# Cross-attention's product with the values in three fp32r passes, the scaling of the probabilities on GpSimd, ScalarE and VectorE reordered

## The reference

```python
q = jnp.einsum('bsd,hdk->bhsk', queries, Wq)      # queries = layernorm(x), 16 heads of 64
k = jnp.einsum('bsd,hdk->bhsk', keys, Wk)         # keys = values = ctx, (4, 77, 256)
v = jnp.einsum('bsd,hdv->bhsv', values, Wv)
scores = jnp.einsum('bhsk,bhtk->bhst', q, k) / jnp.sqrt(DK)
scores = jnp.where(mask[:, None, :, :] == 0, NEG, scores)
weights = jax.nn.softmax(scores, axis=-1)
out = jnp.einsum('bhst,bhtv->bhsv', weights, v)
x = x + out.transpose(0, 2, 1, 3).reshape(B, S, H * DV) @ Wo
```

## Time and profile before

| | us |
|---|---|
| median of 3 runs (lowest to highest) | 1695.28 (1693.06 to 1700.02) |
| the profiled execution, and its span | 1694.84, 1693.1 |
| TensorE, VectorE, ScalarE, GpSimd busy | 1646.5, 1379.5, 1089.0, 401.5 |
| self-attention | 70 to 750 |
| cross-attention, first scores to the last product's start | 846.3 to 1163.4 |
| experts, from the first matmul | 1176.0 to 1693.1 |

### The profile page before, as it was taken

One profiled execution on the slowest core, in us unless ns is written; L12 is line 12 of the kernel. 1 busy time (PEld: TensorE's weight loads), 2 busy tenths in 40 slices (PEclk: granted clock), 3 DMA queues, 4 the chain that ended last, 5 costly groups with the idle time before them and its releaser, 6 DMA issues. The chain is left out here.

```text
span 1693.1 us, 34421 instructions
## 1 busy us (share of the span) xinstructions
PE 1646.5 (97%) x11830; PEld 1086.5 (64%) x11830; DVE 1379.5 (81%) x2604; ACT 1089.0 (64%) x2271; POOL 401.5 (24%) x464
## 2 busy tenths in 40 slices
PE   7899999999999999999999999997999999999998
PEld 3443333333333333358689999996898888888887
DVE  6799999999999999925678899995797666666664
ACT  5348888888888888862577877774335444454442
POOL 2000000000000000023042222222562555555550
PEclk9869999999999999999999999998999999999999
DMA  6602111111111111021311322113725333333335
GB/s 208 211 16 37 34 33 33 31 31 32 31 31 31 31 31 31 3 63 56 122 49 39 109 77 69 52 47 129 236 75 172 57 54 54 56 52 57 51 57 172
DMA packets 85176, 116.80 MB, mean 69 GB/s; under 512 B 19051, under 2 KB 64415, under 8 KB 84415
## 3 DMA queue, kind: packets, MB, share of 16 engines
q1 hardware_dynamic: 67248, 90.95, 19.2%
q0 software_dynamic: 13728, 18.88, 6.8%
q10 hardware_dynamic: 4047, 4.91, 1.0%
HBM read 71.25 MB, written 46.60 MB: 70 GB/s over the span
## 5 line engine op out<-in xcount | busy, mean ns | idle before, releaser
L506 DVE TENSOR_REDUCE half_max<-psA 128x1 f32<-128x512 f32 x1024 | 630.3, 683 | 6.5 <-PE psA L559 4.4
L538 ACT ACTIVATE PT<-psB 128x1024 f32<-128x1024 f32 x512 | 520.4, 1026 | 140.4 <-PE psB L569 140.1
L559 PE MATMUL psA<-KS,QS 48*128 48x512 f32 x1024 | 397.6, 471 | 7.9 <-PEq L104 2.0
L569 PE MATMUL psB<-QS,KS 50*128 50x512 f32 x1024 | 377.8, 457 | 0.1
L588 PE MATMUL psO<-PT,VG 128*32 128x256 f32 x4096 | 321.0, 392 | 0.1
L559 PEld LDWEIGHTS psA<-KS,QS 48*128 48x128 f32 x1024 | 163.4, 191 | 232.5 <-DVE half_max L506 174.2
L588 PEld LDWEIGHTS psO<-PT,VG 128*32 128x32 f32 x4096 | 84.6, 108 | 176.4 <-issue 102.9
L1390 ACT ACTIVATE x_probs<-x_scores,x_neg_max 128x77 f32<-128x77 f32 x512 | 176.3, 357 | 6.7 <-DVE x_neg_max L1293 6.5
L2129 ACT ACTIVATE swd_high<-WD 128x1024 fp32r x71 | 75.3, 1061 | 149.9 <-PE m_psY L1872 149.9
L569 PEld LDWEIGHTS psB<-QS,KS 50*128 50x128 f32 x1024 | 150.9, 186 | 10.7 <-ACT PT L538 9.5
L1872 PE MATMUL m_psY<-swd_high,m_hT 128*128 128x256 f32 x760 | 155.6, 288 | 0.3 <-issue 0.2
(11 more groups left out here) (232 smaller groups left out, 2690.6 us busy)
## 6 DMA issues: line engine op xcount, KB each, us to landing
QS<-q_parts SPq DMA_DIRECT2D x96, 128.0 KB
q_parts<-part SPq DMA_DIRECT2D x16, 512.0 KB, 4.3
mx_kept<-cx_mx SPq DMA_DIRECT2D x8, 616.0 KB, 4.9
cx_mx<-mx_kept SPq DMA_DIRECT2D x4, 1232.0 KB, 7.4
KS<-k_parts SPq DMA_DIRECT2D x32, 128.0 KB
xf_rows<-XF SPq DMA_DIRECT2D x32, 128.0 KB, 1.7
acc<-X SPq DMA_DIRECT2D x32, 128.0 KB, 1.8
xf_turned<-n_xfT SPq DMA_DIRECT2D x32, 128.0 KB, 1.8
```

The costliest lines, as they stand in the source:

```text
L506: dve.tensor_reduce(half_max[:, h * (TB // 2) + t % (TB // 2), n:n + 1], psA[:, bank_of(slot, 2 * v + r), :], axis=AX.X, op=ALU.max).then_ ...
L538: act.activation(PT[:, k % 4, 2 * a:2 * a + 2, :].rearrange("p h n -> p (h n)"), psB[:, u % 2, :, :].rearrange("p a n -> p (a n)"), ACT.Ex ...
L559: pe.matmul(psA[:, bank_of(slot, m), :], QS[top:top + KQ, slot, h // 2, t * P:(t + 1) * P], KS[top:top + KQ, slot, n * HALF:(n + 1) * HALF ...
L569: mm = pe.matmul(psB[:, u % 2, r, :], KS[top:top + KM, slot, c * P:(c + 1) * P], QS[top:top + KM, slot, a, half * HALF:(half + 1) * HALF], ...
```

## The change

1. The product with the values takes high and low parts: `ET[0]`, `ET[1]` (ScalarE's copy, and VectorE's subtraction from PSUM) and `VO[..., part]`, both fp32r, in three passes: high x high, high x low, low x high. The third waits for the low parts (`e_low`).
2. `VO` holds two sequences at a time. In `phase_context` the values of sequences 2 and 3 are copied raw to `VR` (10 units, in turns), and those of 0 and 1 split, the high part by ScalarE, the low one by VectorE behind it (10 units). In `phase_cross` GpSimd splits `VR` into the slot that is free, one or two chunks a step in seven steps, from step 13 on and again from step 21 on.
3. GpSimd scales the probabilities (`scale_probs`): eight heads after VectorE's first reciprocal, eight after its second (`head_sums`), both calls in a row, behind the splitting and ahead of `n_rstd_all`. GpSimd's steps are all unrolled.
4. The softmax scale goes into the keys; the maximum is written negated and taken in the step of the scores, so the small negation goes.
5. VectorE's order in a step: `x_xnT` low ahead of the masked copies; then the low parts of `x_ET`, reciprocal, maximum, `XF`, its statistics, reciprocal. ScalarE: the first six exponentials ahead of the copies `n_xfT` and `x_xnT`, and `x_xnT` ahead of the copies to `x_ET`.
6. `XF` has two buffers in place of 32 and waits for its store and transposition of two tiles ago; the experts' high weights that lay in its place get one of their own.

The diff, cut to its core:

```diff
 phase_context
+        BACKS = [(b, pair) for b in (2, 3, 0, 1) for pair in range(NPK // 2)]
+        RAW = 2 * (NPK // 2)
@@ VectorE
-            for n in range(1, BACK, 2):
+            for n in range(1, RAW, 2):
                 dve.wait_ge(r_done, n + 1)
-                to, source = back(n)
-                dve.tensor_copy(to, source).then_inc(r_in[1], 1)
+                dve.tensor_copy(raw(n), back(n)).then_inc(r_in[1], 1)
+            for n in range(RAW, len(BACKS)):
+                dve.wait_ge(r_in[0], n - RAW // 2 + 1)
+                dve.tensor_tensor(part_of(n, 1), back(n), part_of(n, 0), ALU.subtract).then_inc(r_in[1], 1)
@@ ScalarE
+            for n in range(0, RAW, 2):
+                act.wait_ge(r_done, n + 1)
+                act.activation(raw(n), back(n), ACT.Copy).then_inc(r_in[0], 1)
             act.wait_ge(mx_in, MX_KEPT)
-            for n in range(0, BACK, 2):
+            for n in range(RAW, len(BACKS)):
                 act.wait_ge(r_done, n + 1)
-                act.activation(to, source, ACT.Copy).then_inc(r_in[0], 1)
+                act.activation(part_of(n, 0), back(n), ACT.Copy).then_inc(r_in[0], 1)
 phase_cross
@@ GpSimd
+            def scale_probs(t, half):
+                i, e = t
+                first, last = HEADS[half]
+                pool.wait_ge(recip_done, 2 * i + half + 1)
+                probs = by_head(PX, e)[:, first:last, :]
+                pool.tensor_tensor(probs, probs, over_keys(recip[:, e, first:last]), ALU.mult).then_inc(scaled, 1)
+            def split_values(slot, c):
+                n = slot * NPK + c
+                pool.tensor_copy(VO[:, slot, 0, c, :], VR[:, slot, c, :]).then_inc(vo_split, 1)
+                pool.wait_ge(vo_split, 2 * n + 1)
+                pool.tensor_tensor(VO[:, slot, 1, c, :], VR[:, slot, c, :], VO[:, slot, 0, c, :], ALU.subtract).then_inc(vo_split, 1)
...
+                own_rstd(0, L_Y)
+                if t := tile(L_Y):
+                    slot, j = t[0] // TB - 1, t[0] % TB
+                    if slot in (0, 1) and j < SPLIT_STEPS:
+                        if j == 0:
+                            pool.wait_ge(y_done, TB * (slot + 1))
+                        for c in range(j * NPK // SPLIT_STEPS, (j + 1) * NPK // SPLIT_STEPS):
+                            split_values(slot, c)
+                if t := tile(L_SM):
+                    scale_probs(t, 0)
+                    scale_probs(t, 1)
+                own_rstd(1, L_XF)
@@ TensorE
-                    pe.wait_ge(scaled, at(i, 1, 1))
+                    pe.wait_ge(scaled, at(i, 2, 2))
...
-                    for c in range(NPK):
-                        if c % 4 == 0:
-                            pe.wait_ge(e_in, at(i, 3, c // 4 + 1))
-                        mm = pe.matmul(psY[:, 0, 0:D], ET[:, c, :], VO[:, i // TB, c, :], start=(c == 0), stop=(c == NPK - 1))
+                    for a, b in PRODUCTS:
+                        for c in range(NPK):
+                            if c % 4 == 0 and (a, b) != PRODUCTS[1]:
+                                pe.wait_ge(e_low if a else e_in, at(i, 3, c // 4 + 1))
+                            mm = pe.matmul(psY[:, 0, 0:D], ET[a][:, c, :], VO[:, slot, b, c, :], ...)
@@ VectorE
+            def head_sums(t, half):
+                i, e = t
+                first, last = HEADS[half]
+                dve.wait_ge(exp_done, at(i, XH, last))
+                dve.reciprocal(recip[:, e, first:last], row_sum[:, e, first:last]).then_inc(recip_done, 1)
...
-                    dve.reciprocal(recip[:, :], row_sum[:, e, :]).then_inc(recip_done, 1)
-                    dve.wait_ge(recip_done, at(i, 1, 1))
-                    dve.tensor_tensor(by_head(PX, e), by_head(PX, e), over_keys(recip[:, :]), ALU.mult).then_inc(scaled, 1)
...
+                    for n, (first, tiles) in enumerate(EBANKS):
+                        dve.wait_ge(e_in, at(i, 3, n + 1))
+                        dve.tensor_tensor(ET[1][:, first:first + tiles, :], psE[:, n, 0:tiles * P].rearrange(...),
+                                          ET[0][:, first:first + tiles, :], ALU.subtract).then_inc(e_low, 1)
+                    dve.tensor_reduce(neg_max[:, e, :], by_head(SX, e), axis=AX.X, op=ALU.max, negate=True).then_inc(neg_done, 1)
...
+                        dve.wait_ge(rt_done, at(i, 1, -1))
+                        dve.wait_ge(kept[e], at(i - e, 16, 0))
+                    dve.tensor_scalar(XF[:, e, :], X[:, i, :], n_mean_var[:, 0, e, 0:1], n_rstd[:, e:e + 1],
```

More of the change, by code:

```diff
@@ L910, in _ @@
             pe.wait_ge(padded, 1)
[L911 to L914, removed]
+            for n, (b, pair) in enumerate(BACKS):
+                m = n - BACK_RING
+                if m >= RAW:
+                    pe.wait_ge(r_in[1], m - RAW // 2 + 1)
+                elif m >= 0:
+                    pe.wait_ge(r_in[m % 2], m // 2 + 1)
                 for half in range(2):
@@ L1005, in phase_cross @@
         PX = sb("x_probs", [P, 2, NPK * P])
-        row_max = sb("x_row_max", [P, 2, XH])
         neg_max = sb("x_neg_max", [P, 2, XH])
         row_sum = sb("x_row_sum", [P, 2, XH])
-        recip = sb("x_recip", [P, XH])
-        ET = sb("x_ET", [P, NPK, P])
+        recip = sb("x_recip", [P, 2, XH])
+        ET = [sb(f"x_ET{part}", [P, NPK, P], F32R) for part in range(2)]
         gate = sb("gate_sb", [P, KD, NE])
@@ L1161, in step @@
                         pool.wait_ge(n_rstd_done[n], at(i, 1, 1))
-            staggered(pool, NT, LAGS, step)
+                own_rstd(0, L_Y)
[10 more added lines that the diff above has]
+                own_rstd(1, L_XF)
+            for n in range(NT + max(LAGS)):
+                step(lambda lag, n=n: (n - lag, (n - lag) % 2) if 0 <= n - lag < NT else None)
         @block.tensor
@@ L1322, in step @@
                     dve.sem_inc(T["waited_dve"], 1)
-                    take_stats(0, own, X)
+                    take_stats(0, own, X[:, i, :])
                 for stage in (aggregate, add_eps):
@@ L1400, in step @@
                     act.activation(xfT[:, e, :, :], psX[:, 0, RX].rearrange("p (k n) -> p k n", n=P), ACT.Copy).then_inc(rt_in, 1)
-                exps(range(0, EARLY))
+                if t := tile(L_XT):
+                    i, e = t
+                    act.wait_ge(xt_done, at(i, 1, 1))
+                    if not peeled(i, 2):
+                        act.wait_ge(s_done, at(i, 3, -3))
+                    act.activation(xnT[0][:, e, :, :], psX[:, 0, 0:D].rearrange("p (k n) -> p k n", n=P), ACT.Copy).then_inc(xt_high, 1)
                 if t := tile(L_E):
@@ L1500, in expert_places @@
     T["split"] = []
-    for weight, tokens in (("WG", "X"), ("WU", "XF")):
+    for weight, tokens in (("WG", "X"), ("WU", "WU_high")):
         high, low = (nc.alloc_sbuf_tensor_at(f"m_{place}_split", [P, NE, KD, FI], F32R, offset=T["place"][place])
```

107 lines of the change are left out of this document (57 added, 50 removed).

## The result

| | before | after |
|---|---|---|
| median of 4 runs (lowest to highest), us | 1696.45 (1693.06 to 1700.02) | 1677.06 (1674.02 to 1678.66) |
| ratio of after to before, 95% interval | | 0.9877 (0.9857 to 0.9897) |
| the profiled execution, its span | 1694.84, 1693.1 | 1678.66, 1676.9 |

A forecast was written before the change was run, and what follows sets the result against it. TensorE was taken to set the pace at 9.68 us a tile, then a VectorE-GpSimd loop at 9.3. Terms -10.6 + 2.5 + 1 + 2.3 - 0.7 = -5.5 gave 1690 us, range 1680 to 1707.

The forecast's parts named there:

- The new loop: Cross-attention, through VectorE and GpSimd: 9.15 to 9.38 us a step, 9.3 taken, for 9.68 before; 10.6 us gained.
- C to R: VectorE's part of the loop, start of masked copies (C) to end of second reciprocal (R): 5.92 us.
- TensorE's part: Product with the values: 30 fp32r matmuls take 3.75 us for 4.40, so TensorE's step falls to 9.03 us.
- VectorE's own sum: Cross-attention: VectorE's work per step after the change, 8.69 us, just under TensorE's 9.03.
- R to the next C: GpSimd's part of the loop, second reciprocal's end to next masked copies: scaling, n_rstd_all, memset and handoffs, 3.23 us.
- The port: Small VectorE SBUF operations and GpSimd exclude each other; xn goes first, GpSimd's scaling waits up to 0.23 us.
- Splitting on GpSimd: Cross-attention: six steps with two units of splitting the values delay XF by 0.4 us each, 2.5 us.
- The shared expert's low parts: Cross-attention: three steps with a shared weight's low part on GpSimd lose 0.3 us each, 1 us.
- A (TensorE keeps pace, 1682): Rival, cross-attention: more handoff overlap puts the loop under TensorE's 9.03 us; -13.1 us, 1682 us; chance 0.24.
- B (the port goes to GpSimd): Rival, cross-attention: second scaling gets the port before xn, loop 9.9 us, 1706 us; chance 0.16.
- C (a scaling of 1.56): Rival: GpSimd scales at the subtraction's rate, 1.56 us; loop 9.7 to 9.9 us, about 1704 us; chance 0.16.
- D (late low parts): Rival: VectorE's added subtractions come late for the product's third pass; around no change; chance 0.02, with anything unseen.

The follow-up runs named there:

- experiment 3: Changed kernel with n_rstd_all moved behind the next memset of the scores and n_xfT ahead of the first six exponentials; 1670.59 us, ratio 0.9831.
- experiment 1: Changed kernel with GpSimd's n_rstd_all moved behind the next step's memset of the scores; 1674.69 us, ratio 0.9859.
- experiment 5: Changed kernel with one more one-column GpSimd operation behind n_rstd_all, ahead of the next memset, result unused; 1693.74 us, ratio 0.9987.
- experiment 6: Changed kernel without GpSimd's splitting of the values and TensorE's wait for it; 1679.26 us, ratio 0.9884.
- experiment 2: Changed kernel with ScalarE's copy n_xfT ahead of the first six exponentials again; 1677.62 us, ratio 0.9880.
- experiment 4: Changed kernel with two of the product's three passes, low parts of x_ET not multiplied; 1676.75 us, ratio 0.9885.
- experiment 7: Changed kernel with VectorE's looped part of cross-attention written out step by step; 1676.83 us, ratio 0.9872.

## Why the prediction was wrong

The direction and the loop that binds were right; the gain of the cross stage was less than half of what was measured: -7.8 us, and -20.5 in the trace. The step that failed is the length of the new loop from C to R; with the measured 5.57 in place of 5.92 the prediction's own sum gives 1690 - 28 x 0.35 = 1680.

- **TensorE's part**, 3.75 us for the product and a step of 9.03: measured 3.50 and 8.77 (experiment 3). Twelve fp32r matmuls at 0.125 were the source; these 30 took 0.117 each. (Of the twelve, the first took 0.18, from 1331.55 to 1331.73, and the others 0.12.) In the steps from the tenth on it decided nothing, since TensorE does not bind there. But it widened what was to be had from 0.65 to 0.90 a step, and the nine steps ahead, at 8.44 to 8.99, could be as short as that only by it.
- **VectorE's own sum**, 8.69: too long as well. Where the step is 8.77 (experiment 3), VectorE is busy 181.5 of 200 us, 7.96 a step. It did not bind in either account.
- **The new loop**, "C to R is 1.61 + 1.58 + 0.15 + 1.40 + 0.98 + 0.20 = 5.92 us": this is the step that failed. The loop exists and binds (experiments 1 and 5), but C to R is 5.57 (5.53 to 5.58 in the full steps). Start to start, the copies take 1.53 (taken: 1.61), the low parts 1.52 (1.58), the first reciprocal 0.10 (0.15), the maximum 1.30 (1.40), `XF` with its statistics 0.94 (0.98), and the last reciprocal 0.18 (0.20). The larger terms were read as a record's length, or as the distance to an instruction that had waited, and the reciprocals' 0.15 and 0.20 had no row at all; each was 0.02 to 0.10 too long. The overlap of neighbours, of which the prediction itself says 0.07 to 0.08, was taken off at some of them only.
- **R to the next C**, 3.23 and up to 3.46 with the port: measured 3.42 and 3.53 in turns, with other parts. Scaling to `n_rstd_all` is 1.24 (taken, with the handoff: 1.31), `n_rstd_all` 0.55 and the memset 1.13 as taken. But `n_rstd_all` to the memset is 0.18 and the memset to the copies 0.24 to 0.35, for 0.08 each.
- **The port**, up to 0.23 a step (0.15 taken): `x_xn` started 0.16 ahead of GpSimd's scaling, as forecast, and kept its 0.36. The scaling was not held up but lasted 1.28 instead of 1.22, 0.06 us; behind the last two tiles, where no `x_xn` follows R, it lasted 1.22. With this the loop is 8.99 to 9.09 where 9.3 was taken; the 25 full steps gave 16.5 us where 25 x 0.38 = 9.5 were taken, 7.0 of the 12.7 missed.
- **Splitting on GpSimd**, 2.5 us: nothing (experiment 6). **The shared expert's low parts**, 1 us: nothing in the trace, since the first three steps, in which they lie, lost the product's whole 0.90; no run leaves them out.
- **The first three steps** lost 0.91 each, where 0.38 was taken: another 1.6 us. In the fill there is no `n_rstd_all` in the loop yet, and the steps follow the product's full 0.90. With 7.0, 2.5 and 1.0 this makes 12.1 of the 12.7; the rest is in the drain.
- **The context's end**, 2.3 us: 2.1. **The last product**: 0.9 for 0.7.
- **What was missing**: ScalarE's and TensorE's loop over `n_xfT` at 8.92 (experiments 1, 2 and 3). ScalarE's 156 of 200 us was read as slack; but the new order put six exponentials ahead of a copy that TensorE needs. It did little harm to the number, since the other loop is longer by 0.1, but it hides what either repair would bring.
- **The rivals.** A (TensorE keeps pace, 1682) is nearest in time, and not what happened: TensorE waits in every step, 0.40 us on average ahead of L1240, and a shorter product leaves the full steps as they are (experiment 4). B (the port goes to GpSimd) and C (a scaling of 1.56) are refuted by the rows: `x_xn` 0.36, scaling 1.22 to 1.28. D (late low parts) as well: the 30 matmuls run through in 3.50 us; only where another wait was taken away (experiment 2) does the third pass wait. The range ended at A's time; a TensorE at its measured 3.50 was in none of the cases.

By the Trainium skill (SBUF — State Buffer, "Who interferes with whom") of a VectorE instruction in a 2-port mode and one of GpSimd, whichever issues first gets the shared pair for its whole instruction, and the other is blocked fully. No row tells the mode of `x_xn`; that it can be held, its 1.40 us in the earlier trace rows shows. Here `x_xn` started 0.16 us ahead and was not held, which agrees; but GpSimd's scaling, in the 0.20 us that it shared with `x_xn`, lost 0.06 us and not 0.20. The estimate by proportion from the Trainium skill (GPSIMD Engine Reference, section 3.1) was 1.35 us for the scaling of 616 columns; measured were 1.22 alone, so the row of this kernel (1151 ns for 576 columns) was the better source.

What stays open: why the loop code of VectorE costs 0.1 us at the wait for the memset (experiment 7 shows that it does, not how), and what delays the memset by 0.18 behind `n_rstd_all`. The trace puts the 0.18 down to GpSimd's wait for its own `n_rstd_all`; behind the same kind of wait, `x_rstd` starts only 0.07 behind the memset (1045.99 + 1.13, and 1047.19), so there is more to it. No run has the three-pass product with VectorE's or ScalarE's whole order of before, so what the new orders are worth with it is not shown, but for `n_xfT` (experiment 2). Why the clock fell for longer in the profiled execution of after isn't known.

## What to carry to other kernels

When a change puts work on an engine that waits for another, look for the loop over both engines and price it by distances from start to start, every term, since 0.35 us in a loop of 28 steps is 9.8 us, nearly as much as the 10.6 that were forecast from it. If one loop binds, work out the next ones too: here three lay within 0.3 us (9.04, 8.92, 8.77), so that two moves shortened the cross stage by 3.5 us and nothing alone, but by 7.5 together. Idle time behind a wait in such a loop is free room: 1.2 to 2.4 us of splitting a step cost nothing there, and 0.62 us on the other side of the wait cost 17 us in all.

## What the runs showed of the hardware

- At a granted clock of 1.00, an fp32r matmul of 256 columns took 0.117 us from start to start in a row of 30 in three passes, and 0.125 in the experts' row of twelve; a plain fp32 one 0.44 for its two records.
- GpSimd multiplies 616 columns by a broadcast factor in 1.22 us, VectorE in 0.72 (distance to the next instruction).
- A handoff from GpSimd to VectorE took 0.17 us in written-out code, and 0.24 and 0.35 in turns in a loop of two steps; one from VectorE to GpSimd 0.08 (1053.04 to 1053.12).
- VectorE's maximum over 1232 columns in SBUF (1050.62, 1.39 us) and GpSimd's first scaling (1050.79, 1.22 us) ran beside each other, and neither was held.
